# Four reorderings in a one-core perceiver kernel: where the tensor engine waits for its operands

## What is computed

```python
# cross attention, x1 = layernorm(x), 16 x 64 x 1024; ctx 16 x 1601 x 1024
energy = einsum('bcn,bmn->bcm', x1, ctx)
attn = softmax(energy, -1); attn = attn / (1e-9 + attn.sum(axis=1, keepdims=True))
x_r = einsum('bcm,bmn->bcn', attn, ctx)
# self attention, 8 heads of two score maps each, 64 x 64 causal
q, k, v = xn @ Wq, xn @ Wk, xn @ Wv
o = softmax(q1 k1) v - lam * softmax(q2 k2) v
o = o * rsqrt(mean(o * o) + eps) * g * (1 - lam0);  x = x + o @ Wo
# feed-forward: tern(W) = alpha * sign(W) * (|W| > 0.05 max|W|)
h = gelu(xn @ tern(W1).T + b1);  y = h @ tern(W2).T + b2
x = x + clip(round(y / s), -7, 7) * s,  s = max|y| / 7 + 1e-8
```

## Time and profile before

| | |
|---|---|
| median of three runs | 1420.54 us |
| profiled execution, its own time | 1418.05 us |
| its span in the profile | 1416.2 us |
| PE busy | 1357.6 us, 96% |
| DVE, ACT busy | 820.5 us, 512.7 us |
| mean granted TensorE clock | 0.986 |
| HBM traffic | 345.89 MB, 244 GB/s over the span |

### The profile page before, as it was taken

How to read it: one execution, slowest core, us unless ns; L and a number is a source line. 1 busy time by engine, 2 the same in 40 slices (tenths; PEclk the granted TensorE clock), 3 DMA queues, 4 the chain that set the end, 5 groups by cost and what they waited for, 6 DMA issues and landing times.

```text
span 1416.2 us, 17052 instructions
## 1 busy us (share of the span) xinstructions
PE 1357.6 (96%) x6642; PEld 646.0 (46%) x6642; DVE 820.5 (58%) x1409; ACT 512.7 (36%) x790; POOL 2.4 (0%) x10
## 2 busy tenths in 40 slices
PE   6979999999999969999999999999999999999993
PEld 4535435444454434444555555444444444444441
DVE  3223424234242288787888885765677853566955
ACT  1111203113021122117777774102666665333333
POOL 0000000000000000000000000000000000000000
PEclk9989999999999989999999999999999999999997
DMA  9999999999989687854444436342778761222263
GB/s 383 420 421 420 421 421 422 404 396 410 382 327 404 247 301 263 306 193 149 131 152 164 148 120 267 119 135 89 209 236 240 238 195 41 79 75 78 75 194 126
DMA packets 110719, 347.01 MB, mean 245 GB/s; under 512 B 40624, under 2 KB 55344, under 8 KB 85040
## 3 DMA queue, kind: packets, MB, share of 16 engines
q1 hardware_dynamic: 107472, 334.38, 64.5%
q10 hardware_dynamic: 3168, 11.54, 2.0%
HBM read 304.47 MB, written 41.42 MB: 244 GB/s over the span
## 4 chain that ended last, share of the span: by engine, by line
PE 66%; issue 16%; DVE 9%; DMA 7%; ACT 2%; SPq 0%; DVEq 0%; POOLq 0%; POOL 0%
PE ps L1060 15%; PE ps L841 12%; PE ps L1010 8%; PE ps L751 7%; PE ps L943 6%; PE ps L897 5%; DMA ctx_sb<-in_ctx 5%; PE ps L793 4%; PE ps L772 4%; PE ps L823 2%; DMA w_scan<-in_w2t 1%; PE ps L963 1%; DVE t_out L1326 1%; DMA w_buf<-in_w1t 1%; PE ps L775 1%
## 5 line engine op out<-in xcount | busy, mean ns | idle before, releaser
L1075 PE MATMUL ps<-t_half,hl 128*128 128x512 f16 x896 | 193.7, 379 | 2.2 <-DMA t_half<-t_dram 2.2
L841 PE MATMUL ps<-ctx_sb,attnT 128*64 128x512 f32 (+1 forms) x832 | 183.5, 601 | 4.4 <-DMA ctx_sb<-in_ctx 4.4
L553 ACT ACTIVATE stg<-ps 128x512 f32<-128x512 f32 (+1 forms) x80 | 44.3, 554 | 356.6 <-PE ps L772 312.7
L1075 PEld LDWEIGHTS ps<-t_half,hl 128*128 128x128 f16 x896 | 87.6, 98 | 108.2 <-issue 2.7
L1060 PE MATMUL ps<-x3h,t_buf 128*128 128x512 f16 x512 | 121.0, 379 | 0.0
L1060 PE MATMUL ps<-x3l,t_buf 128*128 128x512 f16 x512 | 120.9, 379 | 0.0
L751 PE MATMUL ps<-ctxT,x1T 128*64 128x512 f32 x512 | 116.4, 599 | 0.6 <-DMA ctxT<-in_ctxT 0.6
L841 PEld LDWEIGHTS ps<-ctx_sb,attnT 128*64 128x64 f32 (+1 forms) x832 | 59.8, 138 | 122.0 <-issue 115.2
L1496 DVE TENSOR_TENSOR hl<-hq,hl 128x512 f16<-128x512 f32 x112 | 76.3, 689 | 66.6 <-ACT hl L683 66.2
L897 PE MATMUL ps<-wv_sb,x2T 128*128 128x512 f32 x256 | 112.0, 596 | 0.0
L1010 PE MATMUL ps<-wo_sb,oT 128*128 128x512 f32 x256 | 111.6, 593 | 0.3 <-ACT oT L633 0.3
(11 more groups left out here) (198 smaller groups left out, 1596.8 us busy)
## 6 DMA issues: line engine op xcount, KB each, us to landing
ctxT<-in_ctxT SPq DMA_DIRECT2D x64, 1024.0 KB, 16.3
ctx_sb<-in_ctx SPq DMA_DIRECT2D x16, 4096.0 KB, 21.8
ctx_sb<-in_ctx SPq DMA_DIRECT2D x16, 2048.0 KB, 11.6
w_scan<-in_w1t SPq DMA_DIRECT2D x32, 512.0 KB, 5.8
w_buf<-in_w1t SPq DMA_DIRECT2D x32, 512.0 KB, 3.7
w_scan<-in_w2t SPq DMA_DIRECT2D x32, 512.0 KB, 5.6
w_buf<-in_w2t SPq DMA_DIRECT2D x32, 512.0 KB, 4.1
t_dram<-t_set SPq DMA_DIRECT2D x16, 1024.0 KB, 6.5
```

Of the source, the lines that this page charges most:

```text
L841: ins = mm(bank(ea + hf)[C * b:C * b + C, :], attnT[0:w, slots[mt], C * b:C * b + C], ctx_sb[0:w, mt, b, hf * BANK:hf * BANK + BANK], star ...
L1075: ins = mm(bank(b), hl[:, r % RING, n, s * P:s * P + P], t_half[:, r % BRING, :], start=(fresh and k == 0 and n == 0), stop=(k == HK - 1 a ...
```

## The change

It has four parts.

1. Tile 1 takes its blocks 8 to 12 by row block as tile 0 does (`SINGLES` for p < 2), with the waits for groups 1 and 2 at steps 4 and 6.
2. The first load of all, blocks 8 and 9 of tile 0, becomes two loads of one block each, with an own semaphore `first_in` for the first; step 0 waits for `first_in` and step 2 for `ctx_in[0]`.
3. In the self attention `turn(h)` and `weigh(h)` move one product later, behind products 3 and 4 in place of 2 and 3.
4. The last eight steps wait for their factors one by one in the first output's round, in place of all eight ahead of it.

```diff
         def pairs(p):
-            return SINGLES if p == 0 else PAIRS
+            return SINGLES if p < 2 else PAIRS
...
                 m0, m1 = N_GROUPS[g][0], N_GROUPS[g][-1] + 1
+                if q == 0 and g == 0:
+                    sp.dma_start(ctx_sb[:, m0, :, :], ctx[q, m0 * P:(m0 + 1) * P]).then_inc(first_in, 16)
+                    m0 += 1
...
-                if e == 0:
+                if e == 0 and p == 0:
+                    pe.wait_ge(first_in, 16)
+                if e == (2 if p == 0 else 0):
                     pe.wait_ge(ctx_in[0], 16 * p + 16)
-                if e == (4 if p == 0 else 0):
+                if e == (4 if p < 2 else 0):
                     pe.wait_ge(ctx_in[1], 16 * p + 16)
-                if e == (6 if p == 0 else 0):
+                if e == (6 if p < 2 else 0):
                     pe.wait_ge(ctx_in[2], 16 * p + 16)
...
             for h in range(H):
-                for m in range(3):
+                for m in range(4):
                     qk_product(h, m)
                 if h:
                     turn(h)
-                qk_product(h, 3)
+                qk_product(h, 4)
                 if h:
                     weigh(h)
-                for m in range(4, 7):
+                for m in range(5, 7):
                     qk_product(h, m)
...
-            for n in range(7 * HK - LAST_K, 7 * HK):
-                operands(n)
             for s in range(4):
                 for n in range(7 * HK - LAST_K, 7 * HK):
+                    if s == 0:
+                        operands(n)
                     product(n, s)
```

More of the change, by code:

```diff
@@ L228, in build @@
         cst_in, small_in, lam_in, x_in = sem("cst_in"), sem("small_in"), sem("lam_in"), sem("x_in")
+        first_in = sem("first_in")
         ctx_in = [sem(f"ctx_in{g}") for g in range(G)]
```

## The result

| | before | after |
|---|---|---|
| median of the runs (us) | 1420.23 (1419.71 to 1421.53, 4 runs) | 1433.91 (1432.94 to 1435.02, 4 runs) |
| profiled execution, own time / span (us) | 1418.05 / 1416.2 | 1435.02 / 1433.2 |
| self attention starts (us) | 626.15 | 626.33 |
| projection behind it starts | 858.14 | 877.65 |
| from there to the end of the span | 558.06 | 555.55 |

The ratio is 1.0095, 95% interval 1.0078 to 1.0113: 13.7 us slower, where 11.1 were forecast. The last three rows cut the two profiled executions into the stretches of the prediction's parts: +0.18 us until the self attention, 251.32 - 231.99 = +19.33 in it, -2.51 behind it. These make 17.0 and not 13.7, since the profiled execution of before lies 2.2 us under its median and that of after 1.1 above: a stretch of a single profile is known to a few us only.

The account below looks back on a forecast made before the run. PE, busy 96% of the span, was taken as the bound, with a longer loop through ACT and the refill bounding the changed heads. -2.6 + 0 + 15.9 - 2.2 = +11.1 us on 1420.54 gave 1431.6 us, range 1426 to 1436.

Parts of the forecast that it names:

- the loop of part 3: Self attention: squares, w_buf refill, ternary, count, exponentials, products, turn, weigh would take 31.79 us a head, above PE's 29.41.
- Part 1, -2.6: Cross attention: the stop at tile 1 goes, but tile 3's third group limits the gain to 1.8 to 3.0 us; 2.6 taken.
- Part 4, -2.2: End of the kernel: the whole 2.24 us stop of PE for a right factor goes; at the least 1.9 us gained.
- Part 3, +15.9: Self attention: 14.3 us over six heads, 3.10 at the first weigh, less 1.48 at the last head.
- rival D: Cross attention: tile 1's gain is nothing, as tile 2 or 3 waits longer and the clock falls; 1434.2 us, chance 0.07.
- Part 2, 0: Start of the cross attention: cost and gain of splitting the first load end at two unchanged waits, at 17.95 and 78.29.
- A: Self attention: ACT's 4.57 us of idle time absorbs the 3.1 us delay, so the kernel gets faster, 1413.4 us; chance 0.06.
- B: Self attention: the load lands sooner and only the shorter loop, without the refill, sets heads of 31.03 us; 1427.0 us, chance 0.12.
- C: Self attention: new stops make the clock fall in every head, 11 us on top, 1442.7 us; chance 0.05.

Follow-up runs that it names:

- e2_rest: The whole change with turn and weigh put back one product earlier, the other three parts kept; 1415.63 us, ratio 0.9968 to the kernel before.
- e4_count_first: The whole change, with ACT's count of weight tile 4h+1 moved ahead of squares; 1416.26 us, ratio 0.9975 to the kernel before.
- e7_no_refill: The kernel before with only turn and weigh one product later, and the refills of w_buf left out; 1427.91 us, ratio 1.0072 to the kernel before.

## Why the prediction was right, and where it was off

The forecast was slower, 1431.6 us in a range of 1426 to 1436; 1433.91 was measured. Its cause, the loop of part 3, holds. That the time is so near is in part luck: by the runs of single parts, part 1 was worth 1.6 us less than forecast and part 4 1.7 more, and the two errors cancel. Stretch by stretch the two profiles differ by 17.0 us, where 11.1 were forecast: +0.18 for -2.6, +19.33 for +15.9, -2.51 for -2.2.

**Part 3, +15.9: right.** Alone it measured +15.8. In the profile of that run the three pieces are +3.13 ahead of the first `squares` (forecast 3.10), +13.84 over the six heads (14.3), and -0.89 at the last head (-1.48, where 0.51 us of "issue" ahead of the projection was not counted). The first piece agrees better than it could be known: from the start of the self attention to the first `squares` the eight profiles with untouched lists there take 43.35 to 44.70 us, and before has 43.38. The heads are steady, 29.4 in all of these. The stops stand where they were forecast, at the scores' second half and at product 2. What remained uncertain is one link: less the refill, the loop is 27.95 us in both profiles (forecast 31.79 - 3.96 = 27.83), and the refill adds 3.66 to 3.90 with part 3 alone and 3.95 to 4.92 in the profile of after, a mean of 3.77 against 4.23. In the heads this is 2.7 of the 19.33 - 16.08 = 3.25 us by which the same edit costs more in that profile; the rest is in the first piece. Why the load takes longer in that execution stays open; each kernel has one profile.

**Part 1, -2.6: the step that failed.** The prediction said that PE can be at most 3.0 us early at tile 3, and kept nearly all of it. The landing did hold at 211.7, as it said, but PE's lead at its arrival was 6.7 us and not 4.7, and 7.3 in the profile of part 1 alone (in these two executions the wait near 78 us ended 1.1 to 1.7 us sooner, and its product took 7.09 or 8.78 us in place of 10.00), and so PE stood for 4.14 us and paid 2.70 more at the lower clock. The sum charged the clock to the stop that was removed (1.59) and not to the one it forecast in its place: PE restarts at 211.92, 2.6 us ahead of 214.51 to the tenth as forecast, and the clock takes 2.7. It is rival D, held at 0.07, with its mechanism and its place. The price at the lower clock isn't always 2.7: with part 1 alone it is 2.74, and in `e2_rest` 1.63, where PE reached the batch behind at 216.77 and so kept 1.5 us up to the convolution. The runs with part 1 alone (1419.09, -2.3 to +0.3 by the interval) show no gain that can be told.

**Part 2, 0: right**, by the run alone (-0.3 us), where what PE gained at 78 us went into the stop at 97.

**Part 4, -2.2: too small.** The profile shows about the forecast, -2.5. The medians show -3.9 (-4.8 to -2.3). The stop sometimes drags the clock down behind it, 1.69 us more, in three of eight profiles and not in that of before; this would make -3.1 on average, within the interval, but that it is the whole reason in the runs without a profile isn't shown. The prediction took "after 2.24 they didn't run slower" as a property of a stop of this length.

**The sum.** The four parts alone measure -1.0 - 0.3 + 15.8 - 3.9 = +10.7 before rounding, where the whole change gave +13.7 (11.1 to 16.0 by its interval). Part 3's own interval is 13.8 to 18.5, so the gap of 3.0 isn't clear of noise. The longer refill would make 0.46 x 6 = 2.8 of it, if it is a property of the combination, which one profile can't say.

**The rivals.** A (slack that absorbs the delay) fell: PE waits for the copy of product 6 in every head. But `e4_count_first` shows how near it lay, one place in ACT's list away. B (the short loop) isn't this kernel, though `e7_no_refill` shows that the loop exists, at 30.82. C (the clock falls in every head) fell. The window of the self attention in the profile of after, with stops of up to 1.8 us in it, has a granted clock of 1.00:

```profile
640.00:850.00 210.00, 193.51 (x1013) 98.35 (x1012) 156.53 (x212) 144.00 (x210) 0.00 (x0) 1.00 0.41 132
```

But C isn't empty. Ahead of the projection PE stops 1.70 us at the scores and 0.51 behind them, the same in after, in `e7_no_refill` and with part 3 alone. In the last of these the clock fell there, to 0.89 from 874 to 889 us, and the projection's first 28 records took 1.57 us longer. After, then part 3 alone:

```profile
877.65 12.26 PE L1016 MATMUL ps<-wo_sb,oT 128*128 128x512 f32 x28 [0.51 <-issue]
```

```profile
874.49 13.83 PE L1010 MATMUL ps<-wo_sb,oT 128*128 128x512 f32 x28 [0.51 <-issue]
```

As to the table loads in the loop, the exponentials start 755.49 - 754.20 = 1.29 us behind the start of theirs, and the instruction ahead of it ends at 753.99 + 0.19 = 754.18. The drain of about 1.38 us that the Trainium skill gives (ScalarE: Activation LUTs, What ACT_TABLE_LOAD costs) doesn't appear here either.

## What to carry to other kernels

Idle time of an in-order engine is slack only for what stands in front of its wait: add up the loop from one hand-over to the next across all engines and the DMA, and compare it with what the busiest engine needs; 28.4 against 29.4 us was one product (3.43 us) from becoming the bound. Where the DMA engines are full, as here, a lead won at one stop can be lost at the next landing unless the order of the loads is changed with it, so try such edits in pairs. And charge the clock to the stop that appears as well as to the one that goes.

## What the runs showed of the hardware

**With full DMA engines a landing was set by the bytes ahead in the queue, not by the issue.** Tile 3's third group landed at 211.5 when issued at 195.7, and at 211.7 when issued at 188.9. In all ten profiles with the old order it landed from 210.1 to 212.2 with issues from 188.3 to 196.9; in the four with the new order it landed from 204.3 to 206.5 with issues from 188.1 to 196.4. The Trainium skill, DMA: Bandwidth & Descriptors, Queues, rings and completion order, says that each engine takes descriptors in the order of its ring. The trace agrees: 15.8 and 22.8 us from issue to the same landing.

**The length of a stop tells only in part what the clock costs behind it.** The 32 records of the weighted sum behind the stop near 78 us, in all fourteen profiles, took 7.09 us (granted clock 1.00 in that of after) behind stops of 1.61, 1.66, 3.24 and 3.43 us. They took 8.5 to 8.8 behind six stops from 3.25 to 4.08, and 9.2 to 10.0 behind four from 4.15 to 4.63 (0.76 from 76 to 90 us in that of before, whose 32 records took 10.00). So 3.24 and 3.25 us cost nothing in one profile and 1.7 in another. Behind the 3.35 us stop ahead of the convolution's products (26 records), the same in every kernel, they took 3.14 us twice, 4.7 to 4.8 ten times, and 5.8 and 6.0 once each. A profile that shows no loss behind a stop is one draw; between the first and the last of these lie 2.8 us that no edit made.
